# A four-layer graph network on one core: the norm between layers 2 and 3 by halves of the nodes, and h of layer 1 by ScalarE

## What is computed

```python
for layer in (0, 1, 2, 3):
    h = jnp.maximum(_layernorm(x), 0.0)
    x = x + ref[layer](h, adj, ...)
# layer 0: eight heads, softmax over all nodes of leaky_relu(S1[i,k] + S2[j,k]), k = clip(edges)
# layer 1: h centred and scaled to norm 1; k = h @ w_k, q = h @ w_q
#          a = adj * softmax(k @ q.T / sqrt(8)), a = a / a.sum(-1); result = (a + a@a/2 + (a@a)@(a@a)/6) @ h
# layer 2: Wh = h @ W; e = leaky_relu(Wh a1 + (Wh a2).T); softmax(e where adj > 0) @ Wh, then elu
# layer 3: v_i = sum over j with adj[i,j] of logmap(h_j, h_i); expmap(v, h)
```

## Time and profile before

| | us |
|---|---|
| three timed runs | 977.32, 978.97, 979.09 |
| median | 978.97 |
| the profiled execution, its own time | 977.81 |
| its span in the trace | 976.0 |
| layer 0 and its preparation | 0 to about 545 |
| between layers 0 and 1 | about 545 to 569 |
| layer 1 | 569 to 725 |
| layer 2 | 725 to 778 |
| between layers 2 and 3 | 778 to 804 |
| layer 3's loop, its end | 804 to 950, 950 to 976 |

### The profile page before, as it was taken

One profiled execution on the slowest core, in us unless ns is written; L12 is line 12 of the kernel. 1 busy time (PEld: TensorE's weight loads), 2 busy tenths in 40 slices (PEclk: granted clock), 3 DMA queues, 4 the chain that ended last, 5 costly groups with the idle time before them and its releaser, 6 DMA issues.

```text
span 976.0 us, 18032 instructions
## 1 busy us (share of the span) xinstructions
PE 883.8 (91%) x7000; PEld 329.1 (34%) x7000; DVE 713.9 (73%) x1178; ACT 548.4 (56%) x964; POOL 535.9 (55%) x662
## 2 busy tenths in 40 slices
PE   6899999999998999999999679899979849999981
PEld 5733222222222222222222522233343334555550
DVE  3655557888888887887878679421559668999996
ACT  2689666666665666666656258100130138878863
POOL 3267659889896898988887110000000007778751
PEclk9679999999998999999999879999979967999995
DMA  8671111111210202111000000000000000000000
GB/s 170 150 140 35 55 59 40 30 70 34 74 39 21 73 27 75 40 60 42 27 14 24 1 1 1 1 1 2 1 0 1 1 0 0 1 1 1 1 1 21
DMA packets 23035, 32.64 MB, mean 33 GB/s; under 512 B 14587, under 2 KB 14715, under 8 KB 21926
## 3 DMA queue, kind: packets, MB, share of 16 engines
q1 hardware_dynamic: 20646, 23.11, 7.8%
q0 software_dynamic: 2304, 8.39, 4.7%
HBM read 38.58 MB, written 1.29 MB: 41 GB/s over the span
## 4 chain that ended last, share of the span: by engine, by line
PE 74%; DVE 18%; issue 4%; ACT 3%; SPq 0%; DMA 0%; POOL 0%; DVEq 0%; ACTq 0%
PE ps L1354 23%; PE ps L1364 11%; PE ps L1536 9%; PE ps L1341 6%; DVE big L501 5%; PE ps L1333 4%; PE ps L1484 3%; PE ps L1574 3%; PE ps L1210 2%; DVE big L885 2%; DVE big L498 2%; PE ps L1618 2%; PE ps L1582 1%; PE ps L1321 1%; DVE big L635 1%
## 5 line engine op out<-in xcount | busy, mean ns | idle before, releaser
L635 DVE COPY_PREDICATED big<-mask,ps 128x512 f32<-128x512 uint8 x512 | 341.3, 729 | 114.8 <-PE ps L1341 110.3
L445 POOL TENSOR_SCALAR big<-big 128x512 f32<-128x512 f32 x512 | 355.5, 711 | 79.0 <-PE ps L1364 77.8
L1064 ACT ACTIVATE ps<-ps 128x512 f32<-128x512 f32 x512 | 268.7, 584 | 144.5 <-PE ps L1333 144.2
L1354 PE MATMUL ps<-big 128*32 128x512 f32 x2048 | 254.7, 602 | 0.0
L475 POOL TENSOR_TENSOR big<-big 128x512 f32<-128x512 f32 x34 | 56.0, 1648 | 263.6 <-ACT big L1151 263.6
L1364 PE MATMUL ps<-big 128*32 128x512 f32 x1024 | 135.4, 601 | 0.0
L1333 PE MATMUL ps<-op_r,op_l 18*128 18x512 bf16 x512 | 112.2, 386 | 6.2 <-DVE big L635 4.5
L1354 PEld LDWEIGHTS ps<-big 128*32 128x32 f32 x2048 | 53.7, 109 | 119.6 <-issue 110.5
L1341 PE MATMUL ps<-op_r,op_l 9*128 9x512 bf16 x512 | 75.0, 389 | 0.4 <-ACT ps L1064 0.2
L1618 PE MATMUL ps<-big 66*128 66x512 f32 (+3 forms) x160 | 69.1, 562 | 3.5 <-DVE big L885 2.2
L501 DVE TENSOR_TENSOR big<-big,mask 128x1024 f32<-128x1024 f32 (+4 forms) x72 | 66.9, 956 | 5.7 <-ACT big L1092 4.2
(11 more groups left out here) (293 smaller groups left out, 1088.5 us busy)
## 6 DMA issues: line engine op xcount, KB each, us to landing
big<-max_scratch SPq DMA_DIRECT2D x8, 1024.0 KB, 4.8
big<-rden_scratch SPq DMA_DIRECT2D x30, 256.0 KB, 3.3
big<-in_adj_dram POOLq DMA_DIRECT2D x12, 512.0 KB, 9.2
op_l<-split_scratch SPq DMA_DIRECT2D x56, 36.0 KB
op_r<-split_scratch SPq DMA_DIRECT2D x56, 36.0 KB
work<-in_adj_dram POOLq DMA_DIRECT2D x2, 512.0 KB, 12.6
h_nat<-in_adj_dram POOLq DMA_DIRECT2D x2, 512.0 KB, 11.9
x_nat<-in_x_dram SPq DMA_DIRECT2D x1, 512.0 KB, 4.9
```

The costliest lines, as they stand in the source:

```text
L445: pool.tensor_scalar(ring[:, k % RING, :], vrow[:, head % 2, i0:i0 + HALF], HUGE, g0[:, head, jt:jt + 1], ALU.min, ALU.max).then_inc(s["ba ...
L635: dve.copy_predicated(ring[:, k % RING, :], mask[:, jt, i0:i0 + HALF], ps[:, slot("tile", k), :])\
L1064: act.activation(ps[:, at_slot, :], ps[:, at_slot, :], ACT.Relu, scale=-1.0).then_inc(s["relus"], 1)
L1354: m = pe.matmul(ps[32 * w:32 * (w + 1), MAIN, :], vp[:, head, jt + w // 2, 32 * (w % 2):32 * (w % 2 + 1)], ring[:, (u + w // 2) % RING, :] ...
```

## The change

Layer 0: the VectorE operations of tile 256 are put at tiles 261 (bias), 277 (row sums) and 293 (centred rows).

Layer 0 to 1: GpSimd no longer makes `h`. ScalarE does, in 16 operations of 128 x 64 (scale and bias for each row), between other work; it also makes six of the twelve query slot copies, the squares of the keys and queries, and half of a copy of the turned queries. VectorE fills part of the wait for the square root with a memset and a small copy. TensorE's small product L1439 comes later.

Layer 2 to 3: all is done for nodes 0 to 1023 (b = 0) and nodes 1024 to 2047 (b = 1) apart. For b = 0, the joins stand before gate 4 of the second pass, and four parts of VectorE's chain before gates 7, 9, 11 and 13; TensorE's `turn_out(0)` follows pair 2, its two sets of turns pair 6, and layer 3's first distances stand between pair 7 and the last denominators. For b = 1 the same pieces stand in layer 3's loop at k = 0 to 7. The tile order of layer 3 begins with the nine tiles that need only nodes 0 to 1023. Column sums are taken by a matmul with a constant where there was a transpose and a reduction. The norm's root is by ScalarE as exp(0.5 ln v). `rden` is -2 times `lhs3` by VectorE; `rdis` is scaled in ScalarE's copy. The constant 1 of elu is subtracted at the end.

```diff
+        def square(j):
+            return [[diagonal(j)]] + [[(jt, j // TB + 1, 0, TB)] for jt in range(j, j + TB)] + \
+                [[diagonal(j + 1), diagonal(j + 3)], [diagonal(j + 2), diagonal(j + TB + 2)], [diagonal(j + TB)],
+                 [diagonal(j + TB + 1), diagonal(j + TB + 3)]]
+        OWN = square(0)
+        TILES3 = OWN + [[(jt, c, 0, TB)] for jt in range(HB) for c in range(BLOCKS // 2, BLOCKS)] + square(HB)
...
-            pool.wait_ge(s["means"], 1)
-            pool.tensor_tensor(h[:, :, 0:D], yr, bc(y_mean), ALU.subtract).then_inc(s["h_copied"], 1)
+            pool.wait_ge(s["relu_ready"], 1)
             pool.memset(k_slot[:, :, ER:P // 2], 0.0)
-            pool.wait_ge(s["h_copied"], 1)
-            pool.wait_ge(s["scaled"], 1)
-            pool.tensor_tensor(h[:, :, 0:D], h[:, :, 0:D], bc(stat[:, 2, :]), ALU.mult).then_inc(s["h_copied"], 1)
             pool.wait_ge(s["kq_parts"], 1)
...
+                if k == TILES0 // 2 + 5:
                     link(tt(x[:, :, :], x[:, :, :], pb[:, :].unsqueeze(1).to_broadcast([P, NT, D]), ALU.add))
+                if k == TILES0 // 2 + 21:
                     link(dve.reduce_sum(stat[:, 0, :], x[:, :, :], AX.X))
+                if k == TILES0 // 2 + 37:
                     ts(stat[:, 7, :], stat[:, 0, :], 1.0 / D, None, ALU.mult)
                     link(dve.scalar_tensor_tensor(work[:, :, :], bc(stat[:, 0, :]), -1.0 / D, x[:, :, :], ALU.mult, ALU.add))
...
+            tt(stat[:, 4, :], stat[:, 1, :], stat[:, 3, :], ALU.max).then_inc(s["ln_var"], 1)
+            dve.wait_ge(s["ln_var"], 2)
+            dve.memset(q_slot[:, :, ER:P // 2], 0.0)
             dve.wait_ge(s["wa_done"], 2)
-            dve.tensor_copy(w2c[:, D:DX], ps[0:D, 5, 5 * D:5 * D + 2]).then_inc(s["wall_ready"], 1)
+            dve.tensor_copy(w2c[:, D:DX], ps[0:D, 4, 5 * D:5 * D + 2]).then_inc(s["wall_ready"], 1)
+            root_of_four(stat[:, 2, :], stat[:, 4, :])
+            dve.scalar_tensor_tensor(y_mean, y_mean, -1.0, stat[:, 2, :], ALU.mult, ALU.mult).then_inc(s["scaled"], 1)
...
             for n, c in enumerate(Q_PART):
-                q_part = kq_part[:, c, :].rearrange("p (t e) -> p t e", t=NT)[:, :, E:2 * E]
-                dve.tensor_copy(q_slot[:, :, n * E:(n + 1) * E], q_part)
-                r = dve.tensor_copy(q_slot[:, :, P // 2 + n * E:P // 2 + (n + 1) * E], q_part)
+                r = dve.tensor_copy(q_slot[:, :, n * E:(n + 1) * E],
+                                    kq_part[:, c, :].rearrange("p (t e) -> p t e", t=NT)[:, :, E:2 * E])
             r.then_inc(s["q_slots"], 1)
...
+            def activate(b):
+                of = rows_of(b)
+                dve.wait_ge(s["den2_turned"], b + 1)
+                link(dve.reciprocal(stat[:, 3, of], ps[:, (4, 7)[b], 0:HB]))
+                dve.wait_ge(s["out_turned"], b + 1)
+                tt(work[:, of, :], ps[:, (0, 6)[b], :].rearrange("p (t d) -> p t d", d=D), wide(stat[:, 3, of]), ALU.mult)\
+                    .then_inc(s["part_in"], 1)
+                dve.wait_ge(s["part_in"], 3 * b + 1)
+                link(dve.scalar_tensor_tensor(x[:, of, :], work[:, of, :], 0.0, x[:, of, :], ALU.max, ALU.add))
+            def center_part(b):
+                of = rows_of(b)
+                dve.wait_ge(s["part_out"], 4 * b + 1)
+                link(dve.scalar_tensor_tensor(x[:, of, :], elu[:, of, :], 1.0, x[:, of, :], ALU.min, ALU.add))
+                link(dve.reduce_sum(stat[:, 0, of], x[:, of, :], AX.X))
+                dve.scalar_tensor_tensor(work[:, of, :], wide(stat[:, 0, of]), -1.0 / D, x[:, of, :], ALU.mult, ALU.add)\
+                    .then_inc(s["part_in"], 1)
+                dve.wait_ge(s["part_in"], 3 * b + 2)
+                ts(h[:, of, 0:D], work[:, of, :], 0.0, None, ALU.max).then_inc(s["part_in"], 1)
+            def variance_part(b):
+                of = rows_of(b)
+                dve.wait_ge(s["part_out"], 4 * b + 2)
+                link(dve.reduce_sum(stat[:, 1, of], elu[:, of, :], AX.X))
+                ts(stat[:, 4, of], stat[:, 1, of], 1.0 / D, LN_EPS, ALU.mult, ALU.add).then_inc(s["ln_var"], 1)
+                dve.wait_ge(s["part_out"], 4 * b + 3)
+                link(dve.reduce_sum(stat[:, 7, of], relu2[:, of, :], AX.X))
+            def norm_part(b):
+                of = rows_of(b)
+                root_of_four(stat[:, 2, of], stat[:, 4, of], of)
+                link(tt(h[:, of, 0:D], h[:, of, 0:D], wide(stat[:, 2, of]), ALU.mult))
+                link(tt(stat[:, 7, of], stat[:, 7, of], stat[:, 2, of], ALU.mult))
+                link(tt(stat[:, 7, of], stat[:, 7, of], stat[:, 2, of], ALU.mult))
+                dve.memset(swapped[:, of, DA:DX], 1.0)
+                dve.tensor_copy(swapped[:, of, D:DA], stat[:, 7, of].unsqueeze(2))
+                dve.tensor_copy(h[:, of, DA:DX], stat[:, 7, of].unsqueeze(2)).then_inc(s["h_ready"], 1)
+            def scaled_part(b):
+                dve.wait_ge(s["g_read_b"], 2 * b + 1)
+                ts(rden[0:DX, b * TW:(b + 1) * TW], lhs3[0:DX, b * TW:(b + 1) * TW], minus2, None, ALU.mult).then_inc(s["g_read"], 1)
...
-                    if b == 1 and jt == 6:
+                    if b == 1 and jt == 4:
                         join_halves(0)
                         join_halves(1)
+                    elif b == 1 and jt == 7:
+                        activate(0)
+                    elif b == 1 and jt == 9:
+                        center_part(0)
+                    elif b == 1 and jt == 11:
+                        variance_part(0)
+                    elif b == 1 and jt == 13:
+                        norm_part(0)
                     dve.scalar_tensor_tensor(w2ring[:, jt % W2R, b * TW:(b + 1) * TW], vrow2[:, b * TW:(b + 1) * TW],
                                              tab2[:, 1, jt:jt + 1], mask[:, jt, b * TW:(b + 1) * TW], ALU.max, ALU.mult)\
...
+                if k == 0:
+                    join_halves(2)
+                    join_halves(3)
+                elif k == 1:
+                    activate(1)
+                elif k == 2:
+                    center_part(1)
+                elif k == 3:
+                    variance_part(1)
+                elif k == 4:
+                    norm_part(1)
+                elif k == 6:
+                    scaled_part(1)
...
+            square(sq2, yr, 1)
             turned_out(2, slice(0, HALF // 2), 1)
-            square(sq1, work, 1)
-            square(sq2, yr, 1)
             root(2)
+            act.wait_ge(s["scaled"], 1)
+            for t in range(NT // 4):
+                act.activation(h[:, t, 0:D], yr[:, t, :], ACT.Identity, bias=y_mean[:, t:t + 1], scale=stat[:, 2, t:t + 1])
+            act.wait_ge(s["kqn_done"], 2)
+            act.activation(spare[0][:, 0:KQ], kq, ACT.Square).then_inc(s["squared"], 1)
+            for t in range(NT // 4, NT // 2):
+                act.activation(h[:, t, 0:D], yr[:, t, :], ACT.Identity, bias=y_mean[:, t:t + 1], scale=stat[:, 2, t:t + 1])
+            act.wait_ge(s["kq_parts"], 1)
+            for n, c in enumerate(Q_PART):
+                r = act.activation(q_slot[:, :, P // 2 + n * E:P // 2 + (n + 1) * E],
+                                   kq_part[:, c, :].rearrange("p (t e) -> p t e", t=NT)[:, :, E:2 * E], ACT.Copy)
+            r.then_inc(s["q_slots"], 1)
+            for t in range(NT // 2, NT):
+                r = act.activation(h[:, t, 0:D], yr[:, t, :], ACT.Identity, bias=y_mean[:, t:t + 1], scale=stat[:, 2, t:t + 1])
+            r.then_inc(s["h_copied"], 1)
...
+            def exp_part(b):
+                act.wait_ge(s["part_in"], 3 * b + 1)
+                act.activation(elu[:, rows_of(b), :], work[:, rows_of(b), :], ACT.Exp).then_inc(s["part_out"], 1)
+            def squares_part(b):
+                of = rows_of(b)
+                act.wait_ge(s["part_in"], 3 * b + 2)
+                act.activation(elu[:, of, :], work[:, of, :], ACT.Square).then_inc(s["part_out"], 1)
+                act.wait_ge(s["part_in"], 3 * b + 3)
+                act.activation(relu2[:, of, :], h[:, of, 0:D], ACT.Square).then_inc(s["part_out"], 1)
+            def root_part(b):
+                of = rows_of(b)
+                act.wait_ge(s["ln_var"], 7 + b)
+                act.activation(stat[:, 5, of], stat[:, 4, of], ACT.Ln).then_inc(s["part_out"], 1)
+                act.wait_ge(s["part_out"], 4 * b + 4)
+                act.activation(stat[:, 5, of], stat[:, 5, of], ACT.Exp, scale=0.5).then_inc(s["ln_std"], 1)
+            def swap_part(b):
+                of = rows_of(b)
+                act.wait_ge(s["h_ready"], 2 + b)
+                act.activation(swapped[:, of, 0:D], h[:, of, 0:D], ACT.Copy).then_inc(s["h2_ready"], 1)
+            def left_part(b):
+                act.wait_ge(s["h_turned"], 4 + b)
+                act.activation(lhs3[0:DX, b * TW:(b + 1) * TW], ps[0:DX, 4 + 2 * b:6 + 2 * b, :].rearrange("p b n -> p (b n)"), ACT.Copy)\
                     .then_inc(s["g_read_b"], 1)
...
```

(58 more changed lines are left out.)

136 lines of the change are left out of this document (54 added, 82 removed).

## The result

The changed kernel took 973.92 us (median of five runs, 972.46 to 974.53) beside 978.08 for the kernel before in the same session: a ratio of 0.995, 95% interval 0.9934 to 0.9967. It is faster, by 4.2 us. The forecast was 964.0 with a range of 958 to 971, so the time lies outside. The profiled execution has a span of 972.2 us against 976.0.

A forecast was written before the change was run, and what follows sets the result against it. Full stages were taken as bound by their fullest engine, chains between them by latency, mostly on VectorE. -5.7 - 3.3 - 18.8 + 14.4 = -13.4 from 977.8 gave 964.4, stated as 964.0 us; range 958 to 971 for 8 in 10.

The forecast's parts named there:

- part 1: Layer 0: splitting the 6.0 us VectorE block into three pieces gives -5.7 us, bounds -6.0 and -2.5.
- the slack of 1.6 us: Layer 0: VectorE can be away 1.6 us before TensorE waits, so pieces stick out by only 0.1 to 0.2.
- part 3b: Layer 3's first tiles: the chain for nodes 1024 to 2047 inside the loop costs +14.4 us, between +9.7 and +20.
- the price of the port: Layer 3's first tiles: about ten added VectorE operations collide with GpSimd's over SBUF, +1.2 us (0 to 3).
- The tail: Layer 3 from tile 7 on: same number of tiles in another order, 0 us with +-2.
- rival (c): Layer 0's pieces each stop TensorE and cost a clock fall: part 1 is -1, total -9, 969 us; chance 0.12.
- Part 2: Layer 0 to 1: h made by ScalarE instead of GpSimd starts the slot transposes 3.3 us sooner, bounds -1.5 and -4.5.
- Part 3a: Layer 2's second pass: it lengthens by 12.2 us, but layer 3's first distance read comes earlier, -18.8 us.
- rival (d): Layer 2's second pass: four TensorE waits drop the clock and hold it at 1.2 GHz; total +3, 981 us; chance 0.03.
- work and waits at full clock: Layer 3, tile 0's read to tile 7's: 33.8 us instead of 24.1 with the clock up, +9.7 us.
- 3.5 of clock: Layer 3's first tiles: after a 7 us TensorE wait in tile 4 the clock stays low until the first products, +3.5 us.
- rival (b): Layers 2 to 3: the move is worth nothing, clock low from first fill tile, collisions 1 to 2 us; 969 us; chance 0.15.

The follow-up runs named there:

- parts 1 and 2: Changed kernel with the old way from layer 2 to 3, so only the edits in layer 0 and layer 0 to 1: 972.94 us, ratio 0.995.
- part 1 alone: Kernel before with only layer 0's VectorE block split into pieces at tiles 261, 277 and 293: 977.95 us beside 978.64, ratio 0.9988.
- the kernel with the short GpSimd operations: Changed kernel with GpSimd's two 512-column subtractions cut to 8 columns in layer 3's first tiles, one exponential there at scale 0: 969.02 us, ratio 0.9913.
- order alone: Kernel before with the new order of layer 3's tiles and nothing else: 977.84 us beside 977.57, ratio 1.0006.
- the kernel with both moves: Changed kernel with layer 0's pieces at tiles 262, 277, 292, 310 and turn_left(1) at tile 5: 960.86 us, ratio 0.9825.

## Why the prediction was wrong, step by step

The stage readings and the sign held. Two steps failed: in part 1 the slack of 1.6 us, read at one place and used for three (4.2 us), and in part 3b the price of the port that VectorE shares with GpSimd, 1.2 us in the sum and some 4.6 in the runs. The tail added 1.6.

**Part 1: -5.7 forecast, -1.45 measured.** The failed step is the slack of 1.6 us. I read it at the old place, tile 256, and used it for tiles 261, 277 and 293 as if every place had it. 256 is 1 more than a multiple of 3, after the third select of its group; of the new places only 277 is. The other two stopped TensorE for 0.93 and 0.88 us, and after the second stop the clock fell (the same edit without that fall gave -3.0 in the trace of parts 1 and 2). This is my rival (c) in its mechanism; I gave it three stops and -1, it was two and -1.45. With the places moved by one tile the same edit gives -6.8, over my bound of -6.0: the block's price by counting groups of matmuls was a little low. In the kernel before, unlike in the one after, a gain of this size in layer 0 was taken back in layer 3's first tiles, where the clock fell sooner (part 1 alone).

**Part 2: -3.3 forecast.** The slot transposes moved from 563.61 to 559.05; less the 1.45 already won, that is -3.1, and the first exponential of layer 1, from 568.90 to 564.03, says -3.4. The cast fell to 0.29 and the small operation to 0.17 us, from the 1.82 and 1.07 of the earlier trace rows. Right, by its own rows. Another 0.5 us lies in that stretch, which I did not count; part 1 alone has it too (191.3 for 191.8). Kernels with the same instructions there took 186.5 to 188.8, so this part is not known to better than about 1 us.

**Part 3a: -18.8 forecast, -18.8 measured** (first distance read 804.43 to 780.18, less the 5.41 won before layer 2; 0.5 of it lies in the first pass, which I had not touched). The number has luck in it. TensorE's first idle time in the pass is 2.90 us as worked out, but the others are 0.59 and 1.12, together 4.6 where I had four of 8.0. Against that stands a fall of the clock that I had not counted: 0.50 from 760 until within 764 to 766, with 3.64 us for the pair of tiles that takes 1.9 at full clock, and 3.08 for denominators that take 1.9. Some 3.4 us less idle and 2.9 of clock cancel. This is rival (d)'s fall at the first wait; it did not hold, so (d) stayed away.

**Part 3b: +14.4 forecast, +18.9 measured.** The sum was 9.7 of work and waits at full clock, 3.5 of clock, 1.2 of port. It can be followed tile by tile: the first read of each tile, in us after that of tile 0. The forecast is the one at full clock; the third row adds up by how much VectorE's operations beside GpSimd were longer than the same ones without it.

| tile | 1 | 2 | 3 | 4 | 5 | 6 | 7 |
|---|---|---|---|---|---|---|---|
| forecast | 4.5 | 9.2 | 13.5 | 18.2 | 25.7 | 29.4 | 33.8 |
| measured | 4.07 | 10.33 | 16.27 | 21.25 | 32.39 | 36.66 | 42.99 |
| port so far | 0 | 1.01 | 2.63 | 2.99 | 4.82 | 4.82 | 5.84 |
| measured less port and forecast | -0.43 | 0.12 | 0.14 | 0.06 | 1.87 | 2.44 | 3.35 |

- The port, 1.2 in my sum, is the term that failed. Seven rows of VectorE's added operations are longer beside GpSimd, by 0.4 to 1.1 us each, the smallest as much as the largest, 5.8 in all. By the runs 3.6 of the first 4.8 count in the stage's length, and the copy's 1.0 besides: some 4.6, 3.4 more than I had. My half of half an operation's wait was the wrong average: by these rows an operation of VectorE's can lose nearly all of GpSimd's 1.27 us.
- The work and waits at full clock held: up to tile 4 the path is within 0.4 us of the forecast once the port is taken off, although the clock was low from about 787 on, in tile 1, and not only from tile 4. It cost nothing that shows there: VectorE was busy for 7.8 of the 8 us from 788 to 796.
- The clock, 3.5 in my sum: the last row of the table grows from tile 5 on, behind the stop, to 3.4, which is a difference and not a measurement. The rows of the transposes above put 1.7 of it at the stop, an estimate. No run keeps it apart in this kernel. My reading that in the kernel before the clock fell at 813 behind a wait of 1.2 us was wrong: it was down over 813 to 814 already, where that wait begins; the wait before that was 0.98.
- TensorE's queue: moving the transposes by one tile gave 3.1. The wait of 7.3 us with tile 5's distances behind it was in my step (802.1 to 809.4), and so in the 9.7 and in the 3.5 of clock; what I did not do is to ask for its own price.

Of the 4.5 us that the stage is over its sum, the port makes all by its rows (5.8 for 1.2) and 3.4 by the runs (4.6 for 1.2). The 1.1 between fits the kernel with the short GpSimd operations, where VectorE stands idle 1.1 us more in this stage: part of what its operations gain turns into a wait, so the terms aren't independent.

Against +18.9 stand the 18.8 of part 3a, so the move between the layers was worth nothing: my rival (b), 969, in its result. Half of its reason came: the clock was low from the first fill tiles, but cost nothing there; the collisions were 4.6 us and not 1 to 2.

**From tile 7 on: 0 forecast, +1.6 measured**, inside my +-2. 0.3 of it is the order of the tiles. The 1.3 at the end isn't explained: order alone does not show it.

Taken together: 4.2 + 4.5 + 1.6, less 0.7 more in layers 0 to 1 and layer 1 than forecast, make the 9.6 us between -13.4 and -3.8. The chances had a fault of their own: (b) and (c) had 0.15 and 0.12 and were priced one at a time, at 969 each. Both came in their result, and both together make 973.5 by my own terms, outside any range that takes one or the other.

## What to carry to other kernels

Slack belongs to a place, not to a loop: where one engine works in groups of three tiles, a piece of 1.2 us is free behind the third and stops the other engine behind the first or second, so read the rows at each place that a piece goes to. When a chain is moved under a full stage, every wait that it brings stands in an in-order queue; look what stands behind it, and put the waiting instruction behind the work that doesn't need it (one line, some 7 us here). An operation that a chain brings beside GpSimd can pay for almost the whole of GpSimd's operation, whatever its own size; take that for the bound. Before a low clock is blamed or treated, see which engine has the busy time in that stretch.

## What the runs showed of the hardware that was not expected

- TensorE, busy without a gap from 800 to 812, stays at a granted clock of 0.50 while it does distance products (66 rows by 128 columns, 512 wide, fp32; windows of parts 1 and 2). With two idle products of 128 x 128 by 512 behind a tile the clock went to 0.74 and then 1.00 (the kernel with both moves). In the first stretch being busy did not bring the clock back; what made the difference is left open.
- A VectorE operation of 8 columns beside GpSimd takes 0.53 to 1.16 us where it takes 0.17 without: for their size, small operations suffer the most from the shared port. Not every operation pays. This reduction began inside an operation of GpSimd's and kept its 0.68 us (kernel after):

```profile
799.07 1.72 POOL L473 TENSOR_TENSOR big<-big 128x512 f32<-128x512 f32 x1 [2.82 <-ACT big L1269]
799.57 0.68 DVE L865 TENSOR_REDUCE stat<-big 128x8 f32<-128x512 f32 x1
```

- The same instructions can fall into or out of step with GpSimd for three tiles (8 to 10): 5.0 or 3.7 to 3.9 us a tile, for a shift of 3 us ahead of them. That this is the port is read from rows (1.83 against 0.76) and was not tested by itself in those tiles.
